# Moving one 512 KB store per image from SyncE's queue to ScalarE's, and three pairs of DMA transposes ahead of another store

## What is computed

```python
# layer 0: linear attention over the pixels, 4 heads of 32
x = x + _L0_conv_ref(_gn(x), g, w_qkv, mem_kv, w_out, b_out)
# layer 1: 3x3 convolution for channels with (j - i) % 4 == 0, 1x1 for the others
x = x + _L1_conv_ref(_gn(x), w3, w1, b, 4)
```

## Time and profile before

| what | value |
|---|---|
| device time, median of 3 runs | 1960.87 us (1960.73 to 1961.2) |
| profiled execution: its time / its span | 1962.26 us / 1960.5 us |
| TensorE busy | 1861.5 us, 95% |
| VectorE / ScalarE / GpSimd busy | 83% / 70% / 67% |
| mean granted TensorE clock | 0.989 of full speed |
| DMA: mean rate, share of the 16 DMA engines' time that the main hardware queue took | 160 GB/s, 75.3% |

### The profile page before, as it was taken

One profiled execution on the slowest core, in us unless ns is written; L12 is line 12 of the kernel. 1 busy time (PEld: TensorE's weight loads), 2 busy tenths in 40 slices (PEclk: granted clock), 3 DMA queues, 4 the chain that ended last, 5 costly groups with the idle time before them and its releaser, 6 DMA issues.

```text
span 1960.5 us, 51383 instructions
## 1 busy us (share of the span) xinstructions
PE 1861.5 (95%) x21521; PEld 993.2 (51%) x21521; DVE 1632.6 (83%) x3108; ACT 1369.6 (70%) x1480; POOL 1311.3 (67%) x729
## 2 busy tenths in 40 slices
PE   3799999999999999999999999999999999999997
PEld 1455554555554555544555544555544555544552
DVE  6778888888888788888888888888888888888874
ACT  4677776776776777766777766777676777766761
POOL 6476767686666676767676767676667686667670
PEclk8989999999999999999999999999999999999999
DMA  6267877887877797877788878787877797877765
GB/s 130 46 139 157 178 165 155 169 176 160 171 164 161 150 180 157 178 164 159 162 181 152 178 162 157 163 181 150 180 160 161 157 182 156 177 165 157 156 145 145
DMA packets 349430, 313.01 MB, mean 160 GB/s; under 512 B 299152, under 2 KB 299920, under 8 KB 341008
## 3 DMA queue, kind: packets, MB, share of 16 engines
q1 hardware_dynamic: 346656, 305.75, 75.3%
q10 hardware_dynamic: 2224, 3.97, 0.8%
q0 software_dynamic: 320, 0.01, 0.0%
HBM read 68.10 MB, written 67.11 MB: 69 GB/s over the span
## 4 chain that ended last, share of the span: by engine, by line
PE 54%; SPq 21%; DVE 18%; DMA 4%; issue 2%; ACT 1%; POOL 0%; ACTq 0%; DVEq 0%; POOLq 0%
PE pair_ps L922 18%; PE pair_ps L904 8%; DVE km L1286 7%; SPq L334 6%; SPq L321 5%; PE pair_ps L913 5%; PE pair_ps L863 4%; SPq L333 4%; DVE u L1283 4%; DVE image L1338 4%; PE pair_ps L885 3%; PE bank_ps L814 3%; DMA replicas<-yg_lo 3%; PE pair_ps L823 3%; SPq L306 2%; SPq L327 2%
## 5 line engine op out<-in xcount | busy, mean ns | idle before, releaser
L922 PE MATMUL pair_ps<-replicas,w_rep 96*32 96x512 f16 x8192 | 490.3, 383 | 18.0 <-DMA replicas<-yg_lo 18.0
L489 POOL TENSOR_TENSOR u_lo<-u,u_hi 128x1024 f16<-128x1024 f32 x128 | 269.9, 2139 | 280.2 <-ACT u_hi L608 280.2
L492 POOL TENSOR_TENSOR exp_kT_lo<-exp_kT,exp_kT_hi 128x1024 f16<-128x1024 f32 x128 | 273.1, 2134 | 192.8 <-ACT exp_kT_hi L620 190.2
L922 PEld LDWEIGHTS pair_ps<-replicas,w_rep 96*32 96x32 f16 x8192 | 201.6, 96 | 279.8 <-issue 76.7
L495 POOL TENSOR_TENSOR u_lo<-exp_q,u_hi 128x1024 f16<-128x1024 f32 x128 | 270.4, 2142 | 25.7 <-ACT u_hi L626 25.2
L608 ACT ACTIVATE u_hi<-u 128x1024 f16<-128x1024 f32 x128 | 135.3, 1057 | 144.5 <-DVE u L1283 137.5
L1338 DVE SCALAR_TENSOR_TENSOR image<-pair_ps,image 128x512 f32<-128x512 f32 x256 | 175.5, 686 | 45.3 <-PE pair_ps L922 41.3
L626 ACT ACTIVATE u_hi<-exp_q 128x1024 f16<-128x1024 f32 x128 | 131.5, 1050 | 109.2 <-DVE exp_q L1325 109.0
L485 POOL TENSOR_SCALAR u<-image,st 128x1024 f32<-128x1024 f32 x128 | 179.3, 1409 | 29.4 <-DVE st L1222 29.4
L863 PE MATMUL pair_ps<-wqk_hi,u_hi 128*128 128x128 f16 x1024 | 181.5, 222 | 0.0
L1325 DVE TENSOR_TENSOR exp_q<-exp_q,pair_ps 128x1024 f32<-128x1024 f32 x128 | 152.9, 1216 | 32.8 <-PE pair_ps L823 29.8
(11 more groups left out here) (184 smaller groups left out, 4500.2 us busy)
## 6 DMA issues: line engine op xcount, KB each, us to landing
image<-in_x SPq DMA_DIRECT2D x256, 256.0 KB, 4.8
out<-image SPq DMA_DIRECT2D x502, 128.0 KB, 2.3
replicas<-yg_hi SPq DMA_DIRECT2D x252, 165.0 KB, 3.7
replicas<-yg_hi SPq DMA_DIRECT2D x252, 107.2 KB, 2.4
replicas<-yg_lo SPq DMA_DIRECT2D x126, 165.0 KB, 4.2
replicas<-yg_lo SPq DMA_DIRECT2D x126, 107.2 KB, 2.3
uT_hi<-u_hi SPq DMA_TRANSPOSE x128, 4.4
uT_lo<-u_lo SPq DMA_TRANSPOSE x128, 4.0
```

The source lines that it names most:

```text
L489: pool.tensor_tensor(px(UL, v), px(U, v), px(UH, v), ALU.subtract).then_inc(ul_ready, 1)
L492: pool.tensor_tensor(KL[:, v % 2], KT[:, v % 2], KH[:, v % 2], ALU.subtract).then_inc(kl_ready, 1)
L922: mm = pe.matmul(conv_ps[32 * r:32 * r + 32, j % 2], w_rep[0:32 * SLOTS, tap, r], rep[:, j * ROWS + dy:(j + 1) * ROWS + dy, dx:dx + SIDE], ...
```

## The change

`store(e, 2)` leaves SyncE's step and is issued by ScalarE, between `high_u(a, 3)` and the wait for `k_max` of `exp_memory`. On SyncE, `turn_u(a, 1)` and `turn_u(a, 2)` now stand ahead of `store(e, 3)`, and `turn_u(a, 3)` ahead of `load(p, 1)`. ScalarE's `square_y(c, 2)` and `square_y(c, 3)` no longer wait for `y_ready` themselves. In several places two waits in a row change places. No arithmetic changes.

```diff
@@ SyncE
                     load(p, 0)
-                if e is not None:
-                    sp.wait_ge(out_ready, at(e, CHUNKS, 6))
-                    store(e, 2)
                 if a is not None:
                     sp.wait_ge(ul_ready, at(a, UNITS, 1))
                     turn_u(a, 0)
+                    sp.wait_ge(ul_ready, at(a, UNITS, 2))
+                    turn_u(a, 1)
+                    sp.wait_ge(ul_ready, at(a, UNITS, 3))
+                    turn_u(a, 2)
                 if e is not None:
                     sp.wait_ge(out_ready, at(e, CHUNKS, 8))
                     store(e, 3)
                 if a is not None:
-                    sp.wait_ge(ul_ready, at(a, UNITS, 2))
-                    turn_u(a, 1)
+                    sp.wait_ge(ul_ready, at(a, UNITS, 4))
+                    turn_u(a, 3)
                 if p is not None and p >= PRELOADED:
...
                     load(p, 1)
-                if a is not None:
-                    sp.wait_ge(ul_ready, at(a, UNITS, 3))
-                    turn_u(a, 2)
-                    sp.wait_ge(ul_ready, at(a, UNITS, 4))
-                    turn_u(a, 3)
@@ ScalarE
+            def store(s, v):
+
+                for r in range(RES):
+                    act.dma_start(out_dram[s, r][:, v * UNIT:(v + 1) * UNIT],
+                                 px(image(s), v)[32 * r:32 * r + 32]).then_inc(stored[v], 16)
+
...
                     high_u(a, 3)
+                if e is not None:
+                    act.wait_ge(out_ready, at(e, CHUNKS, 6))
+                    store(e, 2)
+                if a is not None:
                     act.wait_ge(k_max, at(a, 8, 7))
                     exp_memory()
                 if c is not None:
-                    act.wait_ge(y_ready, at(c, UNITS, 3))
                     square_y(c, 2)
-                    act.wait_ge(y_ready, at(c, UNITS, 4))
                     square_y(c, 3)
@@ TensorE (one of several swapped pairs of waits)
+                    pe.wait_ge(k_max, at(a, 8, 8))
                     pe.wait_ge(ul_ready, at(a, UNITS, 1))
-                    pe.wait_ge(k_max, at(a, 8, 8))
                     keys(a, 0, pair_ps[2])
```

More of the change, by code:

```diff
@@ L369, in step @@
                     if e is not None:
+                        sp.wait_ge(stored[1], at(e, 16 * RES, 16 * RES))
+                    if e is not None:
                         sp.wait_ge(stored[0], at(e, 16 * RES, 16 * RES))
-                    if e is not None:
-                        sp.wait_ge(stored[1], at(e, 16 * RES, 16 * RES))
                     load(p, 0)
-                if e is not None:
-                    sp.wait_ge(out_ready, at(e, CHUNKS, 6))
-                    store(e, 2)
                 if a is not None:
@@ L383, in step @@
                 if a is not None:
-                    sp.wait_ge(ul_ready, at(a, UNITS, 2))
-                    turn_u(a, 1)
+                    sp.wait_ge(ul_ready, at(a, UNITS, 4))
+                    turn_u(a, 3)
                 if p is not None and p >= PRELOADED:
                     if e is not None:
+                        sp.wait_ge(stored[2], at(e, 16 * RES, 16 * RES))
+                    if e is not None:
                         sp.wait_ge(stored[3], at(e, 16 * RES, 16 * RES))
-                    if e is not None:
-                        sp.wait_ge(stored[2], at(e, 16 * RES, 16 * RES))
                     load(p, 1)
-                if a is not None:
-                    sp.wait_ge(ul_ready, at(a, UNITS, 3))
-                    turn_u(a, 2)
-                    sp.wait_ge(ul_ready, at(a, UNITS, 4))
-                    turn_u(a, 3)
                 if c is not None:
@@ L399, in step @@
                     replicate_high(c, 0)
+                    sp.wait_ge(lo_odd, at(c, UNITS // 2, 1))
                     sp.wait_ge(lo_even, at(c, UNITS // 2, 1))
-                    sp.wait_ge(lo_odd, at(c, UNITS // 2, 1))
                     replicate_low(c, 0)
@@ L404, in step @@
                     replicate_high(c, 1)
+                    sp.wait_ge(lo_even, at(c, UNITS // 2, 2))
                     sp.wait_ge(lo_odd, at(c, UNITS // 2, 2))
-                    sp.wait_ge(lo_even, at(c, UNITS // 2, 2))
                     replicate_low(c, 1)
@@ L542, in step @@
                 if c is not None:
+                    pool.wait_ge(hi_ready, at(c, UNITS, 4))
                     pool.wait_ge(yg_ready, at(c, UNITS, 4))
-                    pool.wait_ge(hi_ready, at(c, UNITS, 4))
                     low_y(c, 3)
@@ L1010, in step @@
                     turn_q_max(bank_ps[1])
+                    pe.wait_ge(uT_in[1], at(a, 32, 32))
                     pe.wait_ge(kl_ready, at(a, UNITS, 2))
-                    pe.wait_ge(uT_in[1], at(a, 32, 32))
                     context(a, 1, bank_ps[0])
@@ L1080, in step @@
                 if a is not None:
+                    pe.wait_ge(el_ready, at(a, UNITS, 1))
                     pe.wait_ge(mix_dve, at(a, 7, 7))
-                    pe.wait_ge(el_ready, at(a, UNITS, 1))
                     mix(a, 0, pair_ps[0])
@@ L1096, in step @@
                 if c is not None:
+                    pe.wait_ge(hi_in[1], at(c, 16 * 2 * RES, 16 * 2 * RES))
                     pe.wait_ge(lo_in[1], at(c, 16 * RES, 16 * RES))
-                    pe.wait_ge(hi_in[1], at(c, 16 * 2 * RES, 16 * 2 * RES))
                     conv_ring(c, 3)
@@ L1404, in step @@
                 if c is not None:
+                    dve.wait_ge(hi_ready, at(c, UNITS, 1))
                     dve.wait_ge(yg_ready, at(c, UNITS, 1))
-                    dve.wait_ge(hi_ready, at(c, UNITS, 1))
                     low_y(c, 0)
```

## The result

The changed kernel takes 1999.9 us in the median of 4 runs (1993.23 to 2014.47), beside 1961.03 us before: a ratio of 1.0201, with a 95% interval of [1.0135, 1.0267]. It is about 2% slower, 1.4 to 2.7% by the interval. The forecast was 1942.9 us, 1% faster.

What follows compares the result with a forecast made beforehand. The prediction took TensorE's wait for late-issued low replicas to bound the kernel. Removing it gave -18.0 us, all other terms 0: 1960.87 - 18.0 = 1942.9 us, with an 8-in-10 range of 1939 to 1955.

Steps and rivals of the forecast that it cites:

- The wait that bounded the kernel: TensorE idle before `conv_ring` for low replicas that SyncE issues late; the change was to remove it all, -18.0 us.
- ScalarE: right: Term for four stores issued by ScalarE: 1.9 us by the median, inside 5.48 us of idle time, so 0.
- The failing step: SyncE's second load, behind the transposes: issued at 995.0 instead of 994.80, landing as before, costed at nothing.
- The replay: SyncE's slow step recomputed in the new order: low replicas landed at 1013.0, before TensorE wants them at 1014.5.
- the first rival: Data engines, not SyncE's issue, are late, so replicas go out as late as now: 1960.9 us, chance 0.09.
- Partly: Rival: the second load, directly ahead of the replicas, holds them; half the waits stay, 1952 us, chance 0.12.
- The slower rival: ScalarE's stores are held by transposes; if each waits for a pair, `exp_memory` comes late: 2096 us, chance 0.07.

Runs made afterwards that it cites:

- e3: The changed kernel with the second load moved ahead of the last pair of transposes and the last-quarter store ahead of the third pair: 1944.66 us, ratio 0.99.
- e7: The kernel of e3 with waits in their old order, except the pair before the second load, and ScalarE's two `y_ready` waits back: 1943.41 us, ratio 0.9895.
- e1: The kernel before with only the third-quarter store moved to ScalarE, SyncE's order otherwise kept: 1964.42 us, ratio 1.001.
- e8: The kernel before with only the second load moved behind the transposes of unit 2, all stores on SyncE: 1965.55 us, ratio 1.0013.
- e9: The changed kernel without the third-quarter store on any engine, and without SyncE's wait for it: 1947.5 us, ratio 0.9942.
- e5: The changed kernel with SyncE also waiting until the second load has landed before issuing the replicas: 1997.3 us, ratio 1.016.
- e2: The kernel before with only SyncE's new order of transposes, last store and second load, the third-quarter store staying first on SyncE: 2064.98 us, ratio 1.0511.
- e4: The kernel before with only the swapped pairs of waits and without ScalarE's two `y_ready` waits, all DMAs in their old places: 1968.09 us, ratio 1.0026.
- e11: The changed kernel itself measured once more, on another chip: 2002.73 us, ratio 1.0219.

## Why the prediction was wrong

**The wait that bounded the kernel: right.** It was worth 18.0 us, and it went. e3 and e7 show the forecast's gain: 1961.72 - 1943.41 = 18.3 us in e7, where 18.0 were predicted, with the steps near 58.1 us that it named. Where the gain comes from was seen less well. The store off SyncE's queue alone takes the wait from 18.0 to 14.5 us (e1), one pair of transposes moved ahead of the load takes it to 5.2 us (e8).

**ScalarE: right.** Its four stores take 2.75 us in the step shown, not 1.9, and lie in the idle time, which still ends with `kneg` after 5.48 us. The rival in which they reach past `kneg` did not happen.

**The failing step: "The second load is issued at 995.0 instead of 994.80, and lands as before. I cost both at nothing"**. The sum has no term for this load, and the runs show two things in its place.

First, the time, which is the step that failed. Put on the mark, 995.0 is 6.3 us; measured were 8.8 to 10.3, 9.6 in the mean. The replay took 2.66 us for a pair of transposes, from pairs that ran with no stores of ScalarE's beside them. In the step above the first pair ends 3.0 us before the mark (forecast 3.4), the second at +0.9 (forecast -0.8) and the third at +4.1 (forecast +1.9); the store of 2.1 us and the last pair follow. Pairs of 3.9 and 3.3 us instead of 2.66 make 1.8 of the 2.8 us. e9 shows what it hangs on: without ScalarE's stores the pairs are back to 2.7 us and the load to 7.6 in the mean. The changed kernel's trace has both queues at work on the 16 DMA engines at once: from 1014 to 1017, in the step above, SyncE's packets (q1) sum to 49.0% of their time and ScalarE's (q10) to 65.5%, more than 100% together, so they overlap. It also gives a price: the transposes took 1.74 instead of 1.37 us (low half) with the stores beside them. That the shared engines are the cause is argued, not shown. Of the stores' data I had asked only whether they leave the move without gain, in the first rival, and not what they do to the transposes. The last 1.3 us, between 6.3 and e9's 7.6, stays unexplained in detail; `S3` took 1.98 us to issue in the median there and up to 3.4, where the replay has 1.71.

Second, the slack. I never asked who waits for the load. The trace before had it, in the same step as the earlier trace rows. VectorE's statistics, and TensorE's group means:

```profile
1003.64 2.47 DVE L1192 BATCH_NORM_STATS2 bn<-image 128x6 f32<-128x512 f32 x4 [0.60 <-DMA image<-in_x]
...
1006.56 0.27 DVE L1201 TENSOR_SCALAR st<-st 128x1 f32<-128x1 f32 x1
```

```profile
1007.88 0.34 PE L928 MATMUL bank_ps<-st,same_group 128*128 128x2 f32 x2
```

VectorE already waited 0.60 us for this load. The statistics were done at 1006.83 and TensorE took them at 1007.88. So the load had 1.05 us left in this step, 1.65 us counted from the point where VectorE first asks. The step is a tight one: over the 29 steps the load has 0.9 to 3.4 us left, 2.6 in the mean. At the replay's own 995.0, 0.2 us later, the load would still have been free, so "at nothing" followed from the replayed time; e3 and e7, with the load at 6.6 and 6.7, bear that out. What the row would have shown is how little the replay may err: a load 4 us later, as measured, could not be free.

**The rivals.** None of them was it. "Partly" put the load in front of the replicas as the suspect, and asked what it does to them; e5 shows that they hold the load instead, by 0.6 us at most. The slower rival looked on ScalarE, where nothing happened. The rival that fitted, an important load pushed back behind transposes that nobody waits for, I had closed with "lands as before".

**The clock.** I had no term for it: in the profiled run TensorE is busy 17.7 us longer, and up to 13.7 of them are half rate behind waits. The kernel before had it too, in the 61.9 us step from `pk` at 634.5: 3.8 us over the 58.1, of which 2.0 are the wait for the replicas. From 663 to 667, behind that wait, the granted clock was 0.57 in the mean. I passed that over.

## What to carry to other kernels

When a queue is reordered, list for every DMA that moves back who waits for it and how much slack it has, even if it is not on the chain now: here one load had 2.6 us in the mean, and was put back by 4. Put issues in the order of their deadlines: in one step of the kernel before, TensorE read the transposes some 15 us and more after they could start, while VectorE asks for the load within 2 us of its landing. A transfer that moves to another engine's queue frees issue time (1.73 us of SyncE's per step here), but may slow what runs beside it, as the transposes here (1.74 instead of 1.37 us for a low half), so a replay must take durations from a stretch with that company, or add a margin.

## What the runs showed of the hardware

- Transposes on SyncE's queue, beside 512 KB of stores that ScalarE issued, took 1.74 (changed), 1.92 (e1) and 2.18 us (e3) for the low half in the median, against 1.34 to 1.37 in runs without such stores (before, e2, e4, e9). A store's issue on ScalarE took 0.594 us in the median in the changed kernel's steps, against 0.445 in the drain, the part behind the loop.
- The first pair of transposes behind a load of 1 MB took 5.1 us in the median (before, e1, e8), a pair with nothing such beside it 2.7.
- A wait of TensorE of 1.77 us was followed by over 3 us at a granted clock of 0.50; so were seven more of the 20 waits over 1.5 us in that trace, and the others were not. TensorE was busy longer than before by 4.4 us (e5) with 32.6 us of waits, 15.1 us (e11) with 44.4, 17.7 us (changed) with 51.2 and 47.5 us (e2) with 76.9.
- The changed kernel's runs spread over 21 us (1993.23 to 2014.47), those of e3 and e7, where TensorE hardly waits, over 5 and 3 us.
